# Graph attention and expert kernel: where TensorE's four semaphore updates in the edge loop stand

## The reference

```
logits = (q[dst] * k[src]).sum(-1) / sqrt(16)          # per edge and head
e      = exp(logits - max of the logits of the same target)
out    = sum over the target's edges of v[src] * e, divided by the sum of e
```

## Time and profile before

| | |
|---|---|
| median of 3 runs | 3453.35 us (3451.68 to 3454.72) |
| profiled execution, span (the only time its page gives) | 3819.9 us |
| TensorE matmul busy | 2598.0 us, 68% |
| VectorE busy | 2277.4 us, 60% |
| GpSimd busy | 1847.1 us, 48% |
| ScalarE busy | 1404.8 us, 37% |
| edge loops, from first to last gather issue | 1210.8 and 1211.8 us |

### The profile page before, as it was taken

One profiled execution on the slowest core, in us unless ns is written; L12 is line 12 of the kernel. 1 busy time (PEld: TensorE's weight loads), 2 busy tenths in 40 slices (PEclk: granted clock), 3 DMA queues, 4 the chain that ended last, 5 costly groups with the idle time before them and its releaser, 6 DMA issues. The chain is left out here.

```text
span 3819.9 us, 47527 instructions
## 1 busy us (share of the span) xinstructions
PE 2598.0 (68%) x13194; PEld 2196.2 (57%) x13194; DVE 2277.4 (60%) x3441; ACT 1404.8 (37%) x2768; POOL 1847.1 (48%) x1956
## 2 busy tenths in 40 slices
PE   2446656666666563466666666666658999999999
PEld 1335445555545453344555445445547999899998
DVE  3236666656766672266666666666655655566655
ACT  6212222222222221022222222222226666676665
POOL 6466666666666646666666666666631000000000
PEclk9755666665566665556666666666658999999999
DMA  9344444434444432344444444444420000000000
GB/s 379 100 102 116 113 112 120 116 110 115 118 112 120 113 93 48 84 110 119 121 123 120 122 119 119 124 114 124 120 76 15 21 5 19 23 11 12 20 10 11
DMA packets 364547, 356.12 MB, mean 93 GB/s; under 512 B 58787, under 2 KB 297682, under 8 KB 364454
## 3 DMA queue, kind: packets, MB, share of 16 engines
q1 hardware_dynamic: 191798, 168.12, 14.0%
q0 software_dynamic: 62832, 125.63, 13.4%
q10 hardware_dynamic: 109824, 61.36, 5.4%
HBM read 246.63 MB, written 108.30 MB: 93 GB/s over the span
## 5 line engine op out<-in xcount | busy, mean ns | idle before, releaser
L154 POOL DMA_INDIRECT kv<-kv_table,ix x1664 | 1582.6, 951 | 842.5 <-issue 468.5
L618 DVE TENSOR_TENSOR_SCAN held_q<-mask,held_q,qT 128x512 f32<-128x512 bf16 x208 | 264.1, 1270 | 785.3 <-remote 733.8
L590 PE MATMUL outT<-identity,run_v 128*128 128x128 f32 x832 | 321.7, 387 | 513.6 <-ACT rows L677 434.1
L568 PE MATMUL kT<-identity,kv 128*128 128x128 f32 x832 | 353.6, 427 | 429.7 <-DMA kv<-kv_table,ix 311.1
L590 PEld LDWEIGHTS outT<-identity,run_v 128*128 128x128 f32 x832 | 219.1, 263 | 573.2 <-ACT rows L677 415.0
L662 ACT ACTIVATE drop<-rise 128x512 f32<-128x512 f32 x208 | 130.9, 629 | 935.6 <-DVE rise L638 478.4
L568 PEld LDWEIGHTS kT<-identity,kv 128*128 128x128 f32 x832 | 193.2, 232 | 446.4 <-issue 375.2
L1245 ACT ACTIVATE full_x<-psH_x,offset_x,scale_x 128x448 f32<-128x448 f32 x448 | 333.6, 745 | 260.3 <-PE psH_x L1098 253.0
L1372 DVE TENSOR_TENSOR hid_lo_x<-full_x,hid_hi_x 128x448 fp32r<-128x448 f32 x448 | 276.1, 623 | 253.4 <-ACT hid_hi_x L1245 242.8
L575 PE MATMUL logit<-kq,head_sum 128*128 128x512 f32 x416 | 389.4, 1039 | 22.6 <-issue 15.8
L592 PE MATMUL restT<-pick,top 128*128 128x8 f32 x1664 | 394.5, 310 | 0.0
(11 more groups left out here) (223 smaller groups left out, 5556.6 us busy)
## 6 DMA issues: line engine op xcount, KB each, us to landing
running_sums<-rows ACTq DMA_DIRECT2D x208, 288.0 KB
qz<-q_at_starts SPq DMA_DIRECT2D x208, 256.0 KB
mask<-masks SPq DMA_DIRECT2D x416, 128.0 KB
q_at_starts<-zeros SPq DMA_DIRECT2D x16, 1664.0 KB
kv<-kv_table,ix POOLq DMA_INDIRECT x1664
x_sb<-in_x SPq DMA_DIRECT2D x1, 6272.0 KB
kv_table<-proj SPq DMA_DIRECT2D x14, 448.0 KB
x_x<-in_x POOLq DMA_DIRECT2D x7, 896.0 KB, 5.7
```

What stands on the lines that cost most here:

```text
L154: pool.indirect_dma_start(kv[:, b % UNROLL, j, 2 * HC * s:2 * HC * (s + 1)], None, kv_t, bass.IndirectOffsetOnAxis(ix[:, b, n:n + 1], 0)). ...
L568: pe.transpose(kT[u % 2][:, P * j:P * (j + 1)], kv[:, u, j, 0::2], identity[:, :])
L590: pe.transpose(outT[:, of], run_v[:, u, of], identity[:, :])
L618: dve.tensor_tensor_scan(held_q[:, h, :], mask[:, u, 0, :], qT[:, :], held_q[:, 1 - h, STEP - 1:STEP], ALU.mult, ALU.add).then_inc(q_held, 1)
```

## The change

The increment on the last matmul of each of TensorE's four stages is taken off, and a drain instruction that carries the increment is put behind that matmul. A drain lets TensorE's sequencer go on only when the engine has finished what was issued to it. No wait, no data and no other engine's code changes.

```diff
                         for j in range(TPB):
                             pe.transpose(kT[u % 2][:, P * j:P * (j + 1)], kv[:, u, j, 0::2], identity[:, :])
-                            ins = pe.transpose(qT[:, P * j:P * (j + 1)], qz[:, u, j, :], identity[:, :])
-                        ins.then_inc(kq_turned, 1)
+                            pe.transpose(qT[:, P * j:P * (j + 1)], qz[:, u, j, :], identity[:, :])
+                        pe.drain().then_inc(kq_turned, 1)
...
-                        pe.matmul(logit[:, :], head_sum[:, :], kq[:, u % 2, :], start=True, stop=True)\
-                            .then_inc(logits_ready, 1)
+                        pe.matmul(logit[:, :], head_sum[:, :], kq[:, u % 2, :], start=True, stop=True)
+                        pe.drain().then_inc(logits_ready, 1)
...
                         for j in range(TPB):
-                            ins = pe.transpose(vT[:, P * j:P * (j + 1)], kv[:, u, j, 1::2], identity[:, :])
-                        ins.then_inc(v_turned, 1)
+                            pe.transpose(vT[:, P * j:P * (j + 1)], kv[:, u, j, 1::2], identity[:, :])
+                        pe.drain().then_inc(v_turned, 1)
...
-                            ins = pe.matmul(restT[:, 1, j, :], top[:, u, of], pick[:, :],
-                                            start=True, stop=True)
-                        ins.then_inc(out_turned, 1)
+                            pe.matmul(restT[:, 1, j, :], top[:, u, of], pick[:, :],
+                                      start=True, stop=True)
+                        pe.drain().then_inc(out_turned, 1)
```

## The result

| | median us | runs |
|---|---|---|
| before | 3454.72 | 7 (3451.68 to 3457.61) |
| after | 3471.37 | 7 (3466.61 to 3480.2) |
| after to before | 1.0047 | 95% interval 1.0036 to 1.0058 |

The change makes the kernel 16.6 us (0.47%) slower. The forecast was 3455 us with a range of 3435 to 3500: the range holds it, the likeliest case (no change within 0.2%) did not happen.

A forecast was written before the change was run, and what follows sets the result against it. GpSimd's issue of eight gathers a block was taken to bound the edge loops, hiding the drains there; the median 3453.35 us plus 2 us for the loop ends gave 3455 us, range 3435 to 3500.

The forecast's parts named there:

- the likeliest case: Whole kernel: timed run unchanged within 0.2%, its own range 3447 to 3462 us; chance 0.60.
- The bound and the cover: Edge loops: GpSimd's gathers set 9.88 us a block; TensorE's slot with drains, around 9.2 us, still fits by 0.7.
- TensorE becomes the bound: Every slot of both loops: slot with drains passes 9.88 us, 46 us slower (3501), far end 400 us; chance 0.24.
- A drain's price: Boundaries between TensorE's stages in the edge loops: 0.5 us each, bounds 0.2 and 0.9.
- 2 us in all: Ends of the two edge loops: about four hand-overs from TensorE at 0.1 to 0.5 us make 1 us a loop.
- Nothing is added to GpSimd, ScalarE, VectorE or SyncE: Edge loops: 832 drains replace increments on matmuls, on TensorE only; no DMA moves.
- The reading of the late updates: Edge loops: TensorE's updates, 7 to 11 us late in the profile, are held up by the recorder, absent outside it.
- the 330 us of the prediction: Edge loops: GpSimd's hold-up by late v_turned in the profile, 1.59 us a block beyond the gathers' pace.
- The sign that was to show the recorder at work: Changed kernel's profile: "remote" rows shrink, span falls by 100 us or more, timed runs stay; then lateness was the recorder's.
- late updates are real: Edge loops: timed runs hold the lateness too and drains free the gathers, up to 330 us faster (3125); chance 0.16.
- The change does not do what it says: Edge loops: a drain waits for the same late completion, 3455 us again; chance inside the no-change case.
- The prediction's step from it: Recording stalls: by the skill's rule on throttled engines, the timed runs have no such stall and the forecast stays the same.

The follow-up runs named there:

- with increments: Kernel before with one unused semaphore increment by TensorE's sequencer where each drain would stand, and no drain: 3463.77 us, 1.0027.

## Why the prediction was right in range and wrong in its likeliest case

**The bound and the cover: right on the quick kind.** Eight gathers a block set the loops (10.04 us), TensorE still waits for them in half of the slots, and its longer slot stays below on average: 9.3 us measured, 9.2 forecast, 0.7 to spare both times. Part of that is luck. The slot without drains was put at 7.3 and is 6.6, and the growth at 2.0 and is 2.7. The block was put at 9.88 us by taking 1397.3 us, from a slow chip's profile, off a quick chip's median; on the quick kind all but the loops takes 1371.0 us (3463.0 - 2092.0, with increments), and a block 10.04 to 10.09. The rival "TensorE becomes the bound" did not happen there, though it was near.

**A drain's price: somewhat under.** 0.5 us at each boundary was forecast and 0.43 read at the logits, but the slot grew by 2.7 us for four. Of this 0.9 is new idle time before the four stages ("issue", 89.3 us over 104 slots) and 1.8 is longer busy time (188.4 us), in which the granted clock was 0.55 for 0.66. The forecast named a lower clock and did not price it.

**The run-downs: mis-sized.** Term "2 us in all". From a loop's last gather to the last store the run-downs took 29.4 and 30.1 us with the increments and 32.4 and 32.1 with drains: 5.1 us more. (The prediction says "some 26 us"; its own two figures give 29.4.) The four hand-overs a loop were too few or too cheap.

**The term that was missing.** "Nothing is added to GpSimd, ScalarE, VectorE or SyncE" is true, but the 96 added entries of TensorE's list were costed only where they execute. 96 entries that nothing depends on cost 8.8 and 9.7 us on the timed runs. The sum as the runs give it: 9.7 (list) + 5.1 (run-downs) + 1.4 (loops) = 16.2, of 16.6 measured. The agreement is closer than the evidence: the 9.7 may be 5.5 to 13.1, the 1.4 and 5.1 are differences of single profiles, and with 160 entries more the changed kernel costs 9.9 us in all.

**The reading of the late updates: wrong.** "I think it does not [exist outside the profile]" rested on 366.5 us between the profiled span and the median. That gap was between two kinds of chip: on the slow kind the kernel before takes 3830 us in 34 timed runs. GpSimd's wait there, the 330 us of the prediction, is as long as the 327 us by which the loops of the two kinds differ (1207.9 + 1210.9 against 1044.8 + 1047.2, neither with a drain). The sign that was to show the recorder at work (the "remote" rows shrink, the span falls by over 100 us, the timed runs stay) came true to the letter and was wrong, because the two profiles were of different chips. So the forecast stood by luck: the chip that judged it has no lateness to lose. Of the rivals, "late updates are real" is true of the slow kind in its premise, and its conclusion, a gain, is the reverse of what happened. "The change does not do what it says" named the mechanism (the drain waits for the same completion) and priced it at nothing. The step that fails on the slow kind is that a drain which waits also holds TensorE, and that this costs 344 us where completions come late.

The Trainium skill, "Perfetto Trace Analysis", section "Tensor Engine Instruction (MATMUL, LD_WEIGHTS)", says that the end shown for a matmul is computed, and that the update goes out only once PSUM has acknowledged the writes. The rows agree in so far as a drain of the results lasts up to 15.6 us, 12 over its median of 3.7, and ScalarE gets the update of the one shown 8.3 us behind the last matmul's shown end.

**Left open.** What makes completions late on two chips and not on the third, and whether it is the chip or the time at which it was used. How the place of TensorE's instructions turns into time. Each timed run has its span and clock from records, on both kinds, so recording alone doesn't make the difference; that it plays a part is neither shown nor excluded. The Trainium skill, "NOTIFIC — the notification-queue block", section 7.1, allows records to stall a producer; no run here shows that block. The prediction's step from it, that the timed runs have no such stall, does not follow, as they are recorded too.

## What to carry to other kernels

An update on the last matmul lets TensorE run ahead while its completion is outstanding; a drain turns a late completion into a stall of the engine. In this kernel one such stall a slot was absorbed and four cost 9.1%. An average of spare time is to be read slot by slot too: 0.7 us here was none in half of the slots. Before a gap between a profile and a timed median is explained, see that both come from the same chip. And an edit of a few instructions in a long unrolled list is to be judged against a control with as many idle instructions: here they were more than half of the effect, 9.7 of 16.6 us.

## What the runs showed of the hardware

- The same kernel took 3454.05 us on one chip and 3829.59 and 3832.64 us (10.9 and 11.0% more) on two others, with updates of TensorE 8 to 15 us late in slots of their edge loops (8.3, 11 and 14.5 in the three read above).
- 96 unused instructions more in TensorE's list cost 8.8 and 9.7 us and 256 more (96 of them drains) 9.9 us, the drains' own cost in it, on the quick kind; 192 more cost 33 us on the slow kind.
- With drains between the stages the granted clock of the loops was 0.55 and 0.56 where it was 0.66 and 0.64 without (quick kind), and 0.53 where it was 0.62 and 0.61 (slow kind): a mix of the two levels (1.2 and 2.4 GHz) with more of the lower.
